# A Mamba2 block with a quantised feed-forward: one 128-channel tile over 512 tokens per step in place of four tiles over 128 tokens

## The reference, cut to what matters

```python
proj = hidden_states @ in_proj_w.T
gate, xBC, dt = jnp.split(proj, [INTER, INTER + CONV_DIM], axis=-1)
xBC = silu(causal convolution of xBC with 4 taps per channel + conv_b)
x, Bm, Cm = split(xBC)
# per head and chunk, dt = clip(softplus(dt + dt_bias)), cs = cumsum(dt * A):
scores = (Cc @ Bc.T) * where(tri, exp(cs[l] - cs[s]), 0)
Y = scores @ (x*dt) + exp(cs) * (Cc @ prev_state) + x * D
state = exp(cs[-1]) * state + Bc.T @ (exp(cs[-1] - cs) * x*dt)
yg = y * silu(gate)
rstd = rsqrt(mean(yg**2, over the 1024 channels of the group) + EPS)
out = (yg * rstd * norm_w) @ out_proj_w.T
```

## Time and profile before

| | |
|---|---|
| median of three runs | 1966.69 us |
| profiled execution | 1969.42 us, span 1967.6 us |
| TensorE (PE) busy | 1897.0 us, 96% |
| VectorE busy | 1603.5 us, 81% |
| ScalarE busy | 1322.0 us, 67% |
| GpSimd busy | 1186.8 us, 60% |
| granted TensorE clock, mean | 0.992 |

### The profile page before, as it was taken

The page is one execution under the profiler, slowest core; times in us unless marked ns, Lnnn a source line. Parts: engine busy times, 40 slices in busy tenths (PEclk is TensorE's granted clock), DMA queues, the critical chain, the costliest instruction groups (busy, mean ns, idle before and its releaser), DMA issues.

```text
span 1967.6 us, 32513 instructions
## 1 busy us (share of the span) xinstructions
PE 1897.0 (96%) x9536; PEld 1531.7 (78%) x9536; DVE 1603.5 (81%) x2108; ACT 1322.0 (67%) x2731; POOL 1186.8 (60%) x840
## 2 busy tenths in 40 slices
PE   4799999999999999999999999999999999998998
PEld 3677787877787888878878888888887888777777
DVE  5488888897989798888889798989898888877850
ACT  3677777777777777777777677777767777743320
POOL 2275666565756667566757566657666576645641
PEclk9899999999999999999999999999999999999999
DMA  3433323233323323332433333333323332324432
GB/s 125 136 120 110 115 88 115 95 107 113 109 91 111 117 95 108 108 115 93 141 104 100 105 110 98 110 111 111 117 83 119 108 115 87 123 67 118 128 104 91
DMA packets 121377, 212.75 MB, mean 108 GB/s; under 512 B 13296, under 2 KB 43376, under 8 KB 121264
## 3 DMA queue, kind: packets, MB, share of 16 engines
q1 hardware_dynamic: 116096, 207.90, 33.6%
q10 hardware_dynamic: 5168, 3.67, 0.6%
HBM read 203.66 MB, written 7.86 MB: 108 GB/s over the span
## 4 chain that ended last, share of the span: by engine, by line
PE 79%; DVE 10%; issue 4%; ACT 2%; DMA 2%; POOL 1%; SPq 0%; ACTq 0%; DVEq 0%; POOLq 0%
PE bank L1240 18%; PE bank L1242 18%; PE bank L1241 17%; PE bank L473 9%; PE bank L479 4%; PE bank L524 4%; DVE z L910 3%; PE bank L620 3%; PE bank L533 3%; PE bank L462 2%; DVE lm L878 1%; PE bank L542 1%; DVE q_raw L1077 1%; DMA lm<-cs_d 1%; DVE q_s L1090 1%
## 5 line engine op out<-in xcount | busy, mean ns | idle before, releaser
L910 DVE SCALAR_TENSOR_TENSOR z<-bank,cw,z 128x511 f32<-128x511 f32 (+2 forms) x480 | 358.4, 747 | 60.1 <-ACT z L684 45.3
L705 ACT ACTIVATE lm<-lm,hp 128x128 f32<-128x128 f32 x1024 | 313.3, 391 | 1.6 <-DVE lm L878 0.9
L1186 POOL TENSOR_TENSOR yt<-yt,gate 128x512 f32<-128x512 f32 x128 | 235.5, 1840 | 108.6 <-DVE yt L954 101.1
L1240 PE MATMUL bank<-xn_hi,conv_hi 128*128 128x512 f32 x640 | 270.0, 422 | 20.3 <-DVEq L915 20.3
L1182 POOL TENSOR_TENSOR yt<-yt,xd 128x512 f32<-128x512 f32 x96 | 168.9, 1759 | 200.1 <-DVE yt L961 200.1
L1137 POOL TENSOR_TENSOR conv_lo<-raw_c,conv_hi 128x512 fp32r<-128x512 f32 x160 | 223.7, 1403 | 100.3 <-ACT conv_hi L652 99.5
L684 ACT ACTIVATE z<-bank,cw 128x512 f32<-128x512 f32 x160 | 123.8, 775 | 214.1 <-PE bank L1242 208.8
L1242 PE MATMUL bank<-xn_hi,conv_lo 128*128 128x512 f32 x640 | 253.5, 396 | 0.0
L1241 PE MATMUL bank<-xn_lo,conv_hi 128*128 128x512 f32 x640 | 251.7, 393 | 0.0
L473 PE MATMUL bank<-xdt,lm 128*128 128x64 f32 x2048 | 243.1, 272 | 2.4 <-issue 2.4
L473 PEld LDWEIGHTS bank<-xdt,lm 128*128 128x128 f32 x2048 | 238.8, 192 | 3.4 <-issue 3.4
(11 more groups left out here) (126 smaller groups left out, 4229.1 us busy)
## 6 DMA issues: line engine op xcount, KB each, us to landing
lm<-cs_d SPq DMA_DIRECT2D x128, 512.0 KB, 4.3
raw_c<-w_conv_dram SPq DMA_DIRECT2D x160, 256.0 KB, 3.5
raw_g<-w_gate_dram SPq DMA_DIRECT2D x128, 256.0 KB, 2.6
raw_o<-w_out_dram SPq DMA_DIRECT2D x128, 256.0 KB, 3.0
hp_d<-stage ACTq DMA_DIRECT2D x2, 1536.0 KB, 6.4
hp<-hp_d SPq DMA_DIRECT2D x32, 96.0 KB, 2.6
q_raw<-w1q_dram SPq DMA_DIRECT2D x10, 256.0 KB, 3.3
q_s<-w1s_dram SPq DMA_DIRECT2D x10, 256.0 KB, 3.5
```

The lines of the kernel that those rows point to most:

```text
L705: e = act.activation(lm[s1 % 2][:, j, :], lm[s1 % 2][:, j, :], ACT.Exp, bias=hp[h1][:, Q_CS, c1, j:j + 1])
L910: ins = dve.scalar_tensor_tensor(z[:, pos % 3, d:SEQ], ps_a[job % 2][:, 0:SEQ - d], cw[:, pos, 3 - d:4 - d], z[:, pos % 3, d:SEQ], ALU.mul ...
L1186: pool.tensor_tensor(yt[:, s % 2, :], yt[:, s % 2, :], gate2[:, s % 2, :], ALU.mult).then_inc(yg_done, 1)
L1240: pe.matmul(dst, a_hi, b_hi, start=(i == 0), stop=False)
```

## The change

The work of a step is cut the other way. Step k works on tile k of the group (128 channels, two heads) over all 512 tokens of the sequence, and y has channels on the partitions. The bodies now go group by group with the two sequences inside, so that the gate and output weights are loaded and split once per group and serve both sequences. The following changes with it.

- TensorE: `xdt` (128 tokens by 64 channels) becomes the stationary operand and `lm` the moving one, and the two heads write partitions 0 to 63 and 64 to 127 of one bank. The transposes of `yt` go. C times state and the new state are three products of 128 columns each in every step. The output projection of the 8 tiles adds up in four PSUM banks for a whole body. The sums of squares come by four products with a column of ones at the end of a body. The input projection runs three steps ahead into one bank (`ps_a`), and gate, B, C, B*C, the transposes of B and the sums of squares share one bank (`ps_g`). The products for B and C stand at the end of steps 3 and 4.
- ScalarE: in every step first the eight exponentials, then the weights, then tap 0, `y_hi` (from SBUF, with the norm weight as scale), the square, the silu of the convolution and the silu of the gate, straight from PSUM (before: tanh and a VectorE operation). Products with the norm weight on the output weights go.
- VectorE: `y_lo` from two SBUF operands; x*D is folded into one operation with the diagonal part; the states are advanced by one copy and four small operations that read the product in PSUM; the accumulation into `acc` is four operations once a body; `part` goes.
- GpSimd: one addition on 384 columns, the product with the gate, the lo parts, and a running sum of squares.
- SyncE: a row load brings 2 heads of 4 chunks in place of 8 heads of one; two more loads a step bring exp(cs) for the C*state part (`ec`).

TensorE, the core of its step:

```diff
+                if pv.exists():
+                    pe.wait_ge(st_done, n)
+                    pe.wait_ge(y1_done, n)
+                    fp32_chunks(ps_y, lambda c: state[:, c - 1, :], lambda c: c_t[:, pv.seq, c * P:(c + 1) * P],
+                                range(1, NC)).then_inc(yo_done, 1)
...
+                    wait(pe, taps_x, 3 * m)
...
+                    pe.wait_ge(xdt_done, n + 1)
+                    pe.wait_ge(sc_done, n + 1)
+                    for c in range(NC):
+                        for j in range(2):
+                            mm = pe.matmul(ps_y[HD * j:HD * j + HD, c * P:(c + 1) * P],
+                                           xdt[:, c * P + HD * j:c * P + HD * j + HD], lm[k % 2][:, 2 * c + j, :],
+                                           start=True, stop=True)
...
+                    fp32_chunks(ps_x, lambda c: b_tok[:, c, :], lambda c: xw[:, c * P:(c + 1) * P], range(NC - 1)
+                                ).then_inc(st_mm, 1)
...
+                    pe.wait_ge(lo_done, n)
...
+                        pe.matmul(ps_o[c][:, :], y_hi[:, o], w[0], start=first, stop=False)
+                        pe.matmul(ps_o[c][:, :], y_hi[:, o], w[1], start=False, stop=False)
+                        mm = pe.matmul(ps_o[c][:, :], y_lo[:, o], w[0], start=False, stop=last)
...
+                if k in (3, 4) and nx.exists():
+                    wait(pe, gev_done, TILES * body.n + k + 3)
...
+                    project_bc(nx, k - 3)
...
+                    wait(pe, st_done, n + 1)
+                    for c in range(NC):
+                        mm = pe.transpose(ps_x[:, c * P:(c + 1) * P], xt[:, k1 % 4, c * P:(c + 1) * P], ident[:, :])
```

ScalarE, whose step is `work_a`, `weights`, `work_b`:

```diff
+                if k in (4, 5) and nx.exists():
...
+                    act.wait_ge(bp_done, 2 * nx.n + i + 1)
...
+                    act.activation(z[:, 2, :], ps_g[:, :], ACT.Identity, scale=cw[:, nx.seq, pos, 3:4],
...
+                    act.wait_ge(min_done, m + 1)
+                    for u in range(2 * NC):
+                        e = act.activation(lm[k1 % 2][:, u, :], lm[k1 % 2][:, u, :], ACT.Exp,
...
+                    act.activation(z[:, kx % 2, :], ps_a[:, :], ACT.Identity, scale=cw[:, bd.seq, pos, 3:4],
...
+                    act.activation(y_hi[:, :], yt[:, kp % 2, :], ACT.Copy, scale=nw[:, pv.seq, kp:kp + 1]
...
+                    act.activation((sq_sum if kp == 0 else sq)[:, :], yt[:, kp % 2, :], ACT.Square,
...
+                    silu_x(bd, kx)
...
+                    act.activation(gate[:, kg % 4, :], ps_g[:, :], ACT.Silu).then_inc(gev_done, 1)
```

VectorE, in its order after `xdt`, `xw` and `t0` (C*state times exp(cs)); the accumulation stands in step 1 only:

```diff
+                if k in (4, 5) and nx.exists():
+                    taps(nx, BC_POS[k - 4], 2, ps_g, tap0_b, taps_b, 2 * nx.n + k - 4)
...
+                    for c in range(NC):
+                        t = NC * before.seq + c
+                        dve.scalar_tensor_tensor(acc[:, t, :], ps_o[c][:, :], rstd[:, c:c + 1], acc[:, t, :],
...
+                    dve.wait_ge(exp_done, m + 1)
...
+                    dve.tensor_tensor(heads_lm, heads_lm, gm[:, :, :].unsqueeze(2).broadcast_to((P, NC, 2, CHUNK)),
...
+                    taps(bd, X_POS[kx], kx % 2, ps_a, tap0_x, taps_x, TILES * bd.n + kx)
...
+                    dve.scalar_tensor_tensor(yt[:, k % 2, :], xt[:, k % 4, :], dc[:, body.seq, k:k + 1], ps_y[:, :],
...
+                    dve.scalar_tensor_tensor(y_lo[:, :], yt[:, kp % 2, :], nw[:, pv.seq, kp:kp + 1],
...
+                    dve.tensor_copy(state[:, 0, :], ps_x[:, 0:P]).then_inc(st0_done, 1)
...
+                            ins = dve.scalar_tensor_tensor(
+                                state[:, c, o], state[:, c - 1, o], hp[body.seq][:, Q_CD, k, 2 * c + j:2 * c + j + 1],
...
+                    dve.scalar_tensor_tensor(lm[kr % 2][:, :, :], per_head(hp[bd.seq], Q_CS, kr, NC, CHUNK), -1.0,
```

SyncE, the load for the step after next:

```diff
+                    wait(sp, yd_done, TILES * bd.n + kr - 1)
+                    sp.dma_start(lm[kr % 2][:, :, :].rearrange("p (c j) l -> p c j l", j=2),
```

More of the change, by code:

```diff
@@ L180, in build @@
             if h == 0:
[L181 to L191, removed]
+                acc = alloc(main, "acc", [TT, DIM])
+        sq = alloc(main, "sq", [SEQ])
+        sq_sum = alloc(main, "sq_sum", [SEQ])
+        y_hi = alloc(main, "y_hi", [SEQ], R32)
+        y_lo = alloc(main, "y_lo", [SEQ], R32)
+        yt = alloc(main, "yt", [2, SEQ])
+        t0 = alloc(main, "t0", [NC - 1, CHUNK])
+        ec = [alloc(main, f"ec{i}", [NC - 1, CHUNK]) for i in range(2)]
+        xdt = alloc(main, "xdt", [NC * P])
+        xw = alloc(main, "xw", [(NC - 1) * P])
+        state = alloc(main, "state", [NC - 1, P])
         main.close()
@@ L380, in _ @@
+            for k in range(1, 6):
+                step(FILL, k)
             sp.wait_ge(cs_out, 16)
-            load_row(Body(0, 0, 0), 0)
             sp.wait_ge(hp_out, 16)
-            load_hp(Body(0, 0, 0), 0)
+            load_hp(Body(0, 0, 0))
+            step(FILL, 6)
+            sp.wait_ge(e_out, 16)
             step(FILL, 7)
@@ L743, in work @@
[L743 to L751 removed]
+                    wait(act, o_done, n - 1)
@@ L847, in _, with taps @@
         def _(dve):
-            def step(body, s):
-                n = STEPS * body.n + s
-                c, h = s % NC, s // NC
-                nx = body.plus(1)
-                if s == 3 and nx.exists():
+            def taps(bd, pos, zi, src, ready, done, i):
+                dve.wait_ge(ready, i + 1)
+                for d in range(1, 4):
+                    if d > 1:
+                        dve.wait_ge(done, 3 * i + d - 1)
+                    dve.scalar_tensor_tensor(z[:, zi, d:SEQ], src[:, 0:SEQ - d], cw[:, bd.seq, pos, 3 - d:4 - d],
+                                             z[:, zi, d:SEQ], ALU.mult, ALU.add).then_inc(done, 1)
@@ L855, in step @@
+            def step(body, k):
+                n = TILES * body.n + k
+                nx = body.plus(1)
+                pv, kp = at(body, k, -1)
+                before = body.plus(-1)
+                if k == 1 and before.exists():
+                    dve.wait_ge(ss_mm, before.n + 1)
+                    wait(dve, rv_done, before.n)
+                    dve.tensor_scalar(rstd_sum[:, :], ps_g[:, 0:NC], EPS, None, ALU.add).then_inc(rs_done, 1)
+                if k == 2 and nx.exists():
                     if nx.is_number(0):
@@ L1191, in _ @@
-            weights(FILL, 2)
-            weights(FILL, 3)
-            conv_weights(late_pieces(FILL, 3))
-            for s in range(3, STEPS - 1):
-                weights(FILL, s + 1)
-                work(FILL, s)
-            work(FILL, 7)
+                if pv.exists() and kp > 0:
+                    pool.wait_ge(sq_done, n)
+                    wait(pool, sqa_done, (TILES - 1) * pv.n + kp - 1)
+                    pool.tensor_tensor(sq_sum[:, :], sq_sum[:, :], sq[:, :], ALU.add).then_inc(sqa_done, 1)
@@ L1200, in unpack @@
+                if k == 3 and body.is_number(0):
+                    pool.wait_ge(hp_out, 16 * SEQS)
+                    pool.wait_ge(qt_tr, NQ * SEQS)
+                    pool.memset(acc[:, :, :], 0.0).then_inc(zero_done, 1)
+            for k in range(2, TILES):
+                step(FILL, k)
             def unpack(m, k, rows, parts):
```

1049 lines of the change are left out of this document (466 added, 583 removed).

## The result

The changed kernel takes 2168.0 us (median of four runs, 2159.0 to 2177.4) against 1966.4: ratio 1.102, interval 1.096 to 1.108. The forecast was 2005, the range 1935 to 2060. Slower was right; the size was wrong by 163 us.

The account below looks back on a forecast made before the run. TensorE's queue bounds the kernel now; after the change the VectorE-ScalarE ring, 12.0 us a step against 11.8. Bodies 2.4 us longer, 38 over 16, on 1969.4 give 2007, median 2005; range 1935 to 2060.

Parts of the forecast that it names:

- The smaller pieces of the row load: SyncE's loads of lm rows: cost taken as nothing with DMA at 34%; landing 4.3 us, at most 6.1.
- The decay products: Eight products a step on TensorE with 64 columns standing, 128 moving: taken as 1.73 us, bounds half of that and 7.5.
- The ring: VectorE and ScalarE wait for each other once a step, from minimum through exponentials, taps, y_lo and states: 12.0 us against TensorE's 11.8.
- plain step: A step without the extra work or waits of particular steps in a body: forecast 12.1 us, late row's 0.1 included.
- step 4: ScalarE's tap 0 of B waits for TensorE's last product of step 3, delaying y_lo: 16.4 us against TensorE's 14.5.
- The steps that are not plain: Steps of a body with extra work or waits, priced one by one: body 107.6 us, 2.4 over today.
- Costed at nothing otherwise: Prologue, between 6 us less and 6 more, and drain with feed-forward cover, 0 to 6: both taken as 0.
- Rival 1: The ring hides in slack, plain steps run at 11.8 us: whole kernel 1940 to 1955; chance 0.20.
- Rival 2: Two heads' decay products run at once, TensorE's step falls to 10.9 us: whole kernel 1980; chance 0.05 as the decider.
- Rival 3: Narrow decay products cost more, 16 unhidden loads of about 0.1 us; TensorE's step 13.4, whole kernel 2090; chance 0.14.
- The signs named for being wrong: TensorE idle before output products under 0.2 us a step, or decay products much less or more than 1.73 us.
- what was to be seen: TensorE idle for y_lo, VectorE waiting for exponentials in most steps, about 250 table loads, TensorE busy about 95% in the bodies.

Follow-up runs that it names:

- pad65: The changed kernel with two unused heads behind the 128 in cs, so a row's four 1 KB runs lie 65 KB apart, not 64: 2056.9 us.
- gap1k: The changed kernel with a tile's row as four runs of 1 KB that lie 1.25 KB apart in place of 64 KB: 2058.5 us.
- row4k: The changed kernel with the sums cs stored head by head, so a tile's row is one run of 4 KB per partition: 2047.4 us.
- norow: The changed kernel with the row loads left out after the first two, every other instruction kept: 2041.6 us.
- row_ec: row4k with exp(cs) stored the same way, so a partition's ec is one run of 1.5 KB, not three of 512 bytes: 2037.6 us.
- serial: row_ec with the eight decay products in the order head, then chunk, so neighbours write the same half of the partitions: 2037.0 us.
- fill: row_ec with products by a tile of zeros ahead of the output products on TensorE, 12 in step 4 and 6 in step 5: 2027.7 us.

## Why the prediction was wrong in size

**The smaller pieces of the row load, costed at nothing.** This is the step that failed. "DMA is at 34%" and the landing of 4.3 were read off a load whose source is one run of 4 KB; the new one takes four runs 64 KB apart. It landed after 8.2 us. The distance of the runs is 111 us by pad65 and 110 by gap1k; with the number of pieces it is 121 (row4k), and no row at all gives 126 (norow). With 65 KB in place of 64 the time is 2057, which the range of 1935 to 2060 would just have held. The prediction even had a price ("if the row lands 1 us later each step costs 0.6 more"), for which it gives no working, and which was too high: between row_ec and the changed kernel the row lands 4.3 us later and a body takes 8.7 us more, 0.25 per us and step. It was only never put to use, since the delay itself was taken as nothing. What it lacked was the question of what the address pattern does to a transfer, and a bound from both sides where no row showed the pattern.

**The decay products, 1.73 us.** They took 1.03. The lower end was named: by the Trainium skill (TensorE: Matmul & The Clock Gate, Part 3, packing) products into different column groups run at the same time, and the trace agrees in kind, 1.03 in alternating order against 1.51 in serial, though not by half. But the saving shortened nothing: serial costs nothing, because `y_lo` was as late.

**The ring, 12.0 us.** In row_ec a plain step is 11.7 us (step 2, forecast 12.4): the sum was right within 0.7, by errors that cancel. y1 and `y_lo` are 1.7 us by their means, not 1.54; the states take 1.3 (1214.43 to the end of 1214.74 above, within my bounds); and the table load of the exponentials is not in the ring in 75 of 128 steps, where the exponentials still wait for the minimum after it, since ScalarE starts it right behind the gate's silu, while VectorE is at the states and the minimum:

```profile
1004.95 1.28 ACT L717 ACT_TABLE_LOAD   x1
1007.79 2.45 ACT L717 ACTIVATE lm<-lm,hp 128x128 f32<-128x128 f32 x8 [1.56 <-DVE lm L997]
```

So the 2.66 us a switch of the Trainium skill (ScalarE: Activation LUTs, What ACT_TABLE_LOAD costs) does not appear: the load is 1.28 us, the exponentials start 0.02 behind it where nothing holds them (step 4 below), and in most steps even the load is hidden. The 0.2 us allowed for blocking of `y_lo` was about right: 0.98 on average against 0.74 at the least.

**The steps that are not plain.** row_ec against the forecast, steps 0 to 7 in us, means over the 16 bodies: 13.2 (12.8), 14.4 (13.1), 11.7 (12.4), 14.2 (14.6), 18.0 (16.4), 13.0 (13.2), 12.4 (12.8), 12.3 (12.3). The mechanism of step 4 stood: tap 0 of B waits for the product issued last, and table load and exponentials queue behind it.

```profile
1021.91 0.78 ACT L708 ACTIVATE z<-bank,cw 128x512 f32<-128x512 f32 x1 [5.30 <-PE bank L137]
1022.71 1.28 ACT L717 ACT_TABLE_LOAD   x1
1024.01 2.46 ACT L717 ACTIVATE lm<-lm,hp 128x128 f32<-128x128 f32 x8
```

In the 15 bodies with a next one step 4 takes 18.4, 2.0 more than forecast. Of these 1.2 are the lower clock behind the wait, which the prediction didn't think of (fill); the other 0.8 are the wait, 2.85 us and not 1.8, against some 0.2 us less of work on TensorE. Step 1 is of the same kind, with a wait of 2.1 us: 13.7 at full clock, 15.2 in the 8 bodies where it fell. The last body prepares no next one and takes only 11.8 us for its step 4; the forecast took all 16 alike, which hides a part of the miss.

**Costed at nothing otherwise.** Behind the last `xdt` 10.9 us were added (10.6 in row_ec), where the bounds were 0 to 6. The prediction had one wait for `y_lo` there, as in the earlier trace rows; TensorE waits twice, 2.08 us and then

```profile
1977.67 0.80 PE L546 MATMUL bank<-wout_hi,y_hi 128*128 128x512 f32 x1 [4.96 <-DVE y_lo L970]
```

together 7.0 against 3.3, and 1.0 before the last decay products. By the windows of this stretch in row_ec, 5.7 of its 10.6 us are idle time of TensorE and 4.9 are work (195.3 us busy against 190.4); which work is not traced. Ahead of the first `xdt` it is 6.2 us less, and 9.0 in row_ec, over the bound of 6 as well. That in row_ec the two ends cancel but for 1.6 us, as the forecast had taken them, is luck.

**The rivals.** Rival 1 needs waits to be hidden that are not. Rival 2's mechanism is real, alone it did nothing. Rival 3 is refuted (the products took 1.03 us, and a load of 64 standing columns 137 ns against 192 in the earlier trace rows), although its 2090 is nearer to the time; by its own sum it should have said more, since a step of 13.4 us makes a body of 114.6, 7.0 over the forecast and not 5.5. The signs named for being wrong: the idle time before the output was well over 0.2 us a step, but the decay products were far from 1.73; that sign pointed to a faster kernel and the kernel was slower. Of what was to be seen, the 256 table loads came as forecast, and VectorE waited for the exponentials in 83 of 128 steps; TensorE's share was 88%, not 95.

In sum, of 163 us: the distance of the runs 110 (2168.0 to 2058.5, gap1k), their number 11 (to row4k), the form of the ec loads 10 (to row_ec, within the noise), and 33 for row_ec over the forecast, of which the bodies are 1.6 each, 26 in all.

## What to carry to other kernels

A transfer that is turned to another cut of the same array has a new price even at equal bytes and a queue at a third of its time: look at the distance between the runs it reads, and where runs read by all partitions lie exactly 64 or 128 KB apart, try an array padded by 1 KB. Before a product is made cheaper on the busiest engine, ask what comes in last beside it; here 0.5 us a step off TensorE gave nothing, and three moves in the order of ScalarE and VectorE gave 99. A wait on TensorE can be paid twice, once as idle time and once as products at the lower clock behind it: here behind 10 of 15 waits of 2.8 us, behind none of 1.6.

## What the runs showed of the hardware

- Broadcast loads of four runs of 1 KB: landing 3.9 us at a distance of 1.25 KB, 4.1 at 65 KB, 8.2 at 64 KB (in one kernel), and 4.6 at 1.25 KB, 6.8 at 128 KB (in the other, where one run of 4 KB takes 4.3). The other loads of the kernel suffer with it: the 256 KB of `raw_x` (weights of the input projection) land after 6.4 us in the changed kernel, 4.0 in pad65. What makes the distance slow no run shows.
- A granted clock of 0.54 over 3.7 us behind 2.85 idle us of TensorE in one body, 1.00 in another after the same wait, and 1.00 in all where products with zeros filled it. Waits of 2.8 us were followed by the lower clock in 10 of 15 bodies, of 2.0 to 2.2 us in 8 of 16, of 1.5 to 1.6 us in none (row_ec, steps 4, 1 and 5).
- Eight pairs of products into alternating halves of the partitions take 1.03 us, in the order half by half 1.51.
- `y_lo`, an operation of VectorE with both operands in SBUF, took 0.74 to 1.59 us in row_ec; the taps, with one operand in PSUM, 0.72 to 0.75.
